# The experts' output matmuls as three F32R products of split operands

## What is computed

```python
def _L0_ffn_ref(x, A, B, Wr, br):
    router_logits = jnp.einsum('bsd,hd->bsh', x, Wr) + br
    scores = H * jax.nn.softmax(router_logits, axis=-1)
    low = jnp.einsum('bsd,hrd->bshr', x, A)
    out = jnp.einsum('bshr,hor,bsh->bso', low, B, scores)
    return SCALING * out
...
x = x + _L0_ffn_ref(_layernorm(x, axis=-1), L0_ffn_A, L0_ffn_B, L0_ffn_Wr, L0_ffn_br)
```

## Time and profile before

| | |
|---|---|
| time, median of 3 runs | 1634.19 us (1629.28 to 1638.53) |
| the profiled execution | its span 1627.3 us, 25328 instructions |
| TensorE busy | 1531.8 us (94%) |
| VectorE busy | 1129.6 us (69%) |
| ScalarE busy | 921.9 us (57%) |
| GpSimd busy | 364.1 us (22%) |
| DMA | 360.94 MB, mean 222 GB/s |

### The profile page before, as it was taken

The page is one execution under the profiler, slowest core; times in us unless marked ns, Lnnn a source line. Parts: engine busy times, 40 slices in busy tenths (PEclk is TensorE's granted clock), DMA queues, the critical chain, the costliest instruction groups (busy, mean ns, idle before and its releaser), DMA issues.

```text
span 1627.3 us, 25328 instructions
## 1 busy us (share of the span) xinstructions
PE 1531.8 (94%) x9574; PEld 1169.6 (72%) x9574; DVE 1129.6 (69%) x1782; ACT 921.9 (57%) x1702; POOL 364.1 (22%) x346
## 2 busy tenths in 40 slices
PE   7999999999999988899999999899999999999986
PEld 6567666666666656778798778798877898875554
DVE  7777745888888878644463785974776955636777
ACT  5444345888888776455543656643657644552443
POOL 1645555555433420110002000012000011001000
PEclk8999999999999999899999999999999999999998
DMA  9667677999987945356577766667766667756542
GB/s 371 204 254 243 223 181 229 276 293 284 273 233 197 253 138 189 130 185 223 202 218 233 258 226 221 214 218 232 265 233 221 223 197 237 218 180 213 203 178 104
DMA packets 127609, 360.94 MB, mean 222 GB/s; under 512 B 15744, under 2 KB 45056, under 8 KB 111872
## 3 DMA queue, kind: packets, MB, share of 16 engines
q1 hardware_dynamic: 127200, 359.19, 68.7%
q10 hardware_dynamic: 288, 0.13, 0.0%
HBM read 273.15 MB, written 86.11 MB: 221 GB/s over the span
## 4 chain that ended last, share of the span: by engine, by line
PE 74%; DVE 12%; ACT 6%; DMA 3%; issue 3%; POOL 1%; SPq 0%; DVEq 0%; ACTq 0%; POOLq 0%
PE ps L1921 21%; PE ps L1933 9%; PE ps L693 5%; PE ps L1249 5%; PE ps L1236 4%; PE ps L1272 4%; PE ps L1946 4%; PE ps L1879 3%; PE ps L1864 3%; PE ps L1809 3%; ACT a_p L1378 3%; PE ps L1824 3%; PE ps L1891 3%; DMA p_x<-in_x 2%; PE ps L652 2%
## 5 line engine op out<-in xcount | busy, mean ns | idle before, releaser
L1921 PE MATMUL ps<-m_y_split,m_win 128*128 128x512 f32 x1536 | 372.7, 396 | 2.7 <-issue 2.7
L1921 PEld LDWEIGHTS ps<-m_y_split,m_win 128*128 128x128 f32 x1536 | 284.2, 189 | 63.9 <-issue 7.1
L1308 DVE TENSOR_REDUCE a_negmax<-ps 128x1 f32<-128x640 f32 (+7 forms) x176 | 180.7, 1027 | 61.1 <-PE ps L1239 60.3
L1378 ACT ACTIVATE a_p<-ps,a_negmax 128x128 f32<-128x128 f32 (+7 forms) x256 | 188.5, 750 | 36.0 <-DVE a_negmax L1308 33.8
L1933 PE MATMUL ps<-m_wods,m_y_split 128*128 128x316 f32 x768 | 178.7, 322 | 3.8 <-DVE m_hT L2145 3.4
L2183 ACT ACTIVATE m_turned<-ps 128x512 f32<-128x512 f32 x128 | 75.0, 596 | 160.3 <-PE ps L1809 129.1
L1249 PE MATMUL ps<-ident,a_p 128*128 128x128 f32 x1152 | 157.8, 275 | 2.9 <-DVE a_pT L1321 2.0
L1236 PE MATMUL ps<-a_k,a_q 128*128 128x512 f32 (+3 forms) x384 | 124.4, 403 | 16.7 <-ACT a_p L1378 15.0
L1933 PEld LDWEIGHTS ps<-m_wods,m_y_split 128*128 128x128 f32 x768 | 128.5, 192 | 8.0 <-DVE m_hT L2145 3.7
L1249 PEld LDWEIGHTS ps<-ident,a_p 128*128 128x128 f32 x1152 | 123.5, 141 | 5.4 <-DVE a_pT L1321 3.5
L2341 POOL TENSOR_TENSOR m_scale<-m_scale,mhalf 128x2 f32<-128x2 f32 x16 | 13.0, 813 | 493.5 <-DVE m_scale L2081 493.5
(11 more groups left out here) (250 smaller groups left out, 3095.3 us busy)
## 6 DMA issues: line engine op xcount, KB each, us to landing
m_win<-mlp_in_split SPq DMA_DIRECT2D x128, 512.0 KB, 4.4
m_wods<-mlp_out_split SPq DMA_DIRECT2D x96, 316.0 KB, 3.3
p_xT<-in_xT SPq DMA_DIRECT2D x16, 1024.0 KB, 9.9
p_x<-in_x SPq DMA_DIRECT2D x16, 1024.0 KB, 10.6
a_q<-qk_split SPq DMA_DIRECT2D x64, 256.0 KB, 7.0
a_k<-qk_split SPq DMA_DIRECT2D x128, 128.0 KB, 7.2
mlp_in_split<-a_w_two SPq DMA_DIRECT2D x32, 512.0 KB, 5.5
m_hs<-in_x SPq DMA_DIRECT2D x15, 1024.0 KB, 5.6
```

The source lines that it names most:

```text
L1308: V.tensor_reduce(negmax[:, n % 4, 0:len(units[n][3])], by_head(n, score_banks(n)), AX_X, ALU.max, negate=True).then_inc(max_ready, 1)
L1378: m = S.activation(dst[:, j, :], src[:, j, :], ACT.Exp, bias=negmax[:, n % 4, j:j + 1], accum_out=rsum[:, si % 2, q * 4 + hh:q * 4 + hh + 1])
L1921: m = nc.tensor.matmul(bank_of("m", blk, step), win[s][:, wl, ic, :], y[k], start=(ic == 0 and p3 == 0), stop=(ic == HCH - 1 and p3 == 2))
```

## The change

The output matmul becomes three F32R matmuls into the same bank: copy times copy, copy times rest, rest times copy. `wB` is loaded to `wB_raw` and split once by VectorE, after its part of the last turn of block 0, into `wB_hi` and `wB_lo` (which takes the place of `wB_raw`). Per tile the turned low-rank values are split into `lT` and `lT_lo` by two VectorE instructions, which read PSUM; ScalarE's copy is gone. The places in `order` stay as they are. TensorE waits for the split weights instead of for the load. The program is made with a DMA descriptor scratch of 1024 bytes.

```diff
+        wB_hi = sb("e_B_hi", [P, D], F32R)
+        lT_lo = [sb(f"e_lowT_lo{k}", [P, P], F32R) for k in range(2)]
...
-        wB = sb("e_B", [P, D])
+        start = place[0]
+        wB_raw = sb("e_B", [P, D])
+        place[0] = start
+        wB_lo = sb("e_B_lo", [P, D], F32R)
...
-        lT = [sb(f"e_lowT{k}", [P, P]) for k in range(2)]
+        lT = [sb(f"e_lowT{k}", [P, P], F32R) for k in range(2)]
...
-                pe.wait_ge(eB_loaded, 32)
+                pe.wait_ge(tables_ready, EXPERTS)
                 wait_for_emptied(pe, "e", i, "lowT")
                 wait_for_bank(pe, "e", i, "out", q)
-                nc.tensor.matmul(bank_of("e", i, "out", q), lT[i % 2][:, :], wB[:, 512 * q:512 * q + 512],
-                                 start=True, stop=True).then_inc(eout_mm, 1)
+                for p3, (l, w) in enumerate(((lT, wB_hi), (lT, wB_lo), (lT_lo, wB_hi))):
+                    m = nc.tensor.matmul(bank_of("e", i, "out", q), l[i % 2][:, :], w[:, 512 * q:512 * q + 512],
+                                         start=(p3 == 0), stop=(p3 == 2))
+                m.then_inc(eout_mm, 1)
...
+            if part == "lowT":
+                dve.wait_ge(elwT_mm, i + 1)
+                dve.wait_ge(eout_mm, 4 * (i - 1))
+                c = dve_own.then_inc(V.tensor_copy(lT[i % 2][:, :], bank_of("e", i, "lowT")[:, 0:P]))
+                dve.wait_ge(dve_own.sem, c)
+                V.tensor_tensor(lT_lo[i % 2][:, :], bank_of("e", i, "lowT")[:, 0:P], lT[i % 2][:, :].bitcast(F32),
+                                ALU.subtract).then_inc(one.sem(("e", i, "lowT")), 1)
...
+        def split_experts():
+            dve.wait_ge(eB_loaded, 32)
+            V.tensor_copy(wB_hi[:, :], wB_raw[:, :]).then_inc(tables_ready, 1)
+            dve.wait_ge(tables_ready, EXPERTS - 1)
+            V.tensor_tensor(wB_lo[:, :], wB_raw[:, :], wB_hi[:, :].bitcast(F32), ALU.subtract).then_inc(tables_ready, 1)
...
                     turn_dve(i, q)
+                    if (i, q) == (0, 7):
+                        split_experts()
...
-            if part == "lowT":
-                act.wait_ge(elwT_mm, i + 1)
-                act.wait_ge(eout_mm, 4 * (i - 1))
-                S.activation(lT[i % 2][:, :], bank_of("e", i, "lowT")[:, 0:P], ACT.Copy).then_inc(
-                    one.sem(("e", i, "lowT")), 1)
...
-    nc = bacc.Bacc("TRN2", target_bir_lowering=False, num_devices=1)
+    nc = bacc.Bacc("TRN2", target_bir_lowering=False, num_devices=1, dynamic_dma_scratch_size=1024)
```

More of the change, by code:

```diff
@@ L532, in program @@
         MHALF, ONES1, ZEROS = 1, 2, 2
-        READ1, WSUM, WQ, MASKS, READ2, ASUM = 3, 4, 5, 7, 8, 9
+        READ1, WSUM, WQ, MASKS, READ2, EXPERTS = 3, 4, 5, 7, 8, 10
         sums_mm = sem("sums_mm")
@@ L2441, in mix_sp @@
                 elif what == "t" and (i, q) == (0, 0):
-                    move(wB[:, :], expB).then_inc(eB_loaded, 16)
+                    move(wB_raw[:, :], expB).then_inc(eB_loaded, 16)
                     move(brb[:, :], br.unsqueeze(0).broadcast_to([P, NE])).then_inc(eB_loaded, 16)
```

## The result

The changed kernel took **1643.79 us** (median of 5 runs, 1640.88 to 1646.23) and the kernel before 1634.19 (1629.28 to 1638.54 in 5 runs beside them): the ratio is 1.0064, with a 95% interval of 1.0042 to 1.0086. That is slower by 9.6 us in medians. The forecast was 1639.2 us, with most of its chance on "no difference" (slower by over 0.5% had 0.28); the result lies inside the whole range of 1627 to 1648 us, on its upper side, and 0.6 us above the forecast's own +0 to +9 us.

What follows compares the result with a forecast made beforehand. TensorE bounds 835 to 1570 us, VectorE to 1607; -7.1 + 3.5 + 1.0 + 0.6 + 0.5 + 6.2 + 0.3 = +5.0 us on the 1627.3 us span, plus 6.9 to the median: 1639.2 us, range 1627 to 1648.

Steps and rivals of the forecast that it cites:

- products, tiles 0 to 11: Output matmuls on TensorE: 41 of 48 outputs stand where TensorE is last and save 0.173 us each, -7.1 us.
- tile 2, stop and clock: TensorE waits near 1080 us for VectorE's late copy, +3.5 us; half of a 2.1 us half-speed loss behind it, +1.0.
- tile 1, tiles 5 and 6: Copies on VectorE ahead of existing TensorE waits: +0.6 us for tile 1, +0.5 us for tiles 5 and 6 together.
- tail: Last tiles: copies lengthen VectorE's work, tile 13's late copy stops TensorE and its clock falls; +6.2 us, bounds 1.2 to 8.
- split of the weights: VectorE's one-time split near 699 us fits its idle time beside GpSimd's subtractions: +0.3 us, between 0 and 2.
- layout, scratch: Smaller descriptor scratch and shifted SBUF addresses cost nothing.
- sum: All terms together: +5.0 us on the profiled span, giving 1639.2 us, +0.3%.
- rival 2: Late VectorE copies: both stops cost their clock in full, tiles 5 and 12 stop too; +10 us, 1644 us, chance 0.20.
- the prediction's own signs: In the changed profile: TensorE stops near 1080 and 1600 us, none above 0.5 behind 699, 1 to 2 ahead at 1570.
- rival 4: At the MLP's start the split and GpSimd's subtractions hold each other up; TensorE stands 2 us, 1641 us, chance 0.10.

Runs made afterwards that it cites:

- e3: The changed kernel with its F32 output matmul back and the weights unsplit, VectorE still making copy and rest: 1647.62 us beside 1635.31, ratio 1.0066.
- e5: The changed kernel with the weights' split cut into four pieces behind MLP steps of block 0: 1643.03 us beside 1634.20, ratio 1.0050.
- e1: The kernel before with the 1024-byte descriptor scratch and the new tiles laid out but unused: 1634.64 us beside 1635.31, ratio 0.9995.
- e4: The changed kernel with the two VectorE copy instructions of tiles 2, 13 and 15 earlier in VectorE's order: 1635.66 us beside 1635.31, ratio 0.9997.
- e8: The changed kernel with 12 unused matmuls ahead of tiles 2 and 13's first output, into the output's own bank: 1647.17 us beside 1634.20, ratio 1.0072.
- e9: The changed kernel with 12 unused matmuls ahead of tiles 2 and 13's first output, into the free down-product bank: 1639.88 us beside 1634.86, ratio 1.0035.
- e2: The kernel before with split weights and three products, ScalarE's copy kept and reused in the third (output wrong): 1632.24 us beside 1635.31, ratio 0.9973.

## Why the prediction came out as it did

By its own steps, predicted against the ledger:

| step | predicted | measured |
|---|---|---|
| products, tiles 0 to 11 | -7.1 | -4.4 (after against e3) |
| tile 2, stop and clock | +3.5 and +1.0 | +5.2 (e3; after +5.0: 3.4 and 1.6) |
| tile 1, tiles 5 and 6 | +0.6 and +0.5 | -0.1 and +0.7 (e3) |
| tail | +6.2 | +8.0 (after), +6.5 (e5), +7.5 (e3) |
| split of the weights | +0.3 | +1.7 |
| layout, scratch | 0 | 0 (e1) |
| 710 to 970 us, with the clock near 900 us | none | +0.7 |
| sum | +5.0 | +11.9 in the ledger; +9.6 in medians |

**The mechanism was right.** Both stops are where the prediction put them, for the reason it gave: 3.34 us at tile 2 (said 3.5) and 6.08 at tile 13 (said 5 to 6), both ended by the rest on VectorE, which stands in a stretch without a gap. e4 takes away the place alone and with it 8 to 11 us. Tiles 5 and 12, which rival 2 had stop as well, don't: only three waits at L1897 are for it, the third is tile 15's, 1.39 us. Of the prediction's own signs two failed: the wait behind the split was 1.40 us, where none above 0.5 was expected, and at 1570 us TensorE was not 1 to 2 us ahead of before but 3.9 behind (6.19 less the 2.3 of the start).

**The products were over-counted, not over-priced.** The term was 41 outputs by 0.173. One output saves 0.16 (1.29 - 1.14 gives 0.15, the matched instructions 0.15 to 0.18). 41 x 0.16 would be 6.6; 4.4 arrived. Matching against e3 says where it went, for the 47 outputs between 970 and 1569 us:

- Around tile 1's four (1000 to 1053 us) the changed kernel gains nothing and loses 0.5 us to e3. Its half-speed stretch comes behind the wait at 1043 us (clock 0.63 over 1044 to 1048 us), while e3 has 1.00 there.
- The four of tile 10 (1522 to 1535 us) gave 0.07 us together: the two waits behind them, 0.37 and 0.66 us before, are 0.67 and 0.84.
- Eight more gave nothing: one each near 1086, 1232, 1274 and 1315 us, and both near 1286 and 1480. The waits at 1285 and 1287 us grew from 0.78 and 1.24 us to 0.96 and 1.40, the one at 1318 from 0.43 to 0.74, and behind 1274 one of 0.30 us is new; near 1086, 1232 and 1480 no such wait is to be seen, and why nothing was gained there stays open.
- The other 31 at 0.16 are 5.0 us, less the 0.5 of tile 1.

The prediction knew the long VectorE stretches (7 outputs lost) and missed the short ones. Nor did the prediction see that at tile 1 the turn L1814 needs the bank of the low-rank values, and so waits 1.54 us for L2130; the later wait for L2060 gives most of that back (2.66 us, before 3.80).

**Clock.** At tile 2 I took half of 2.1; 1.6 came in the changed kernel and 2.7 in e5. In every profiled execution with a bare stop of 3.3 us there (after, e3, e5, e8) the clock was at half speed behind it. The full price is the likelier of the two for this stop, and rival 2's half of the argument was the better one. It is no law for every stop: near 900 us all eleven profiled executions have a stop of 2.73 us, and the clock fell behind it in four (after, e4, e8, e9) and in none of the other seven. Those four are among the five that run the whole split at 702 us beside GpSimd (e2 is the fifth). Whether the split has to do with it, 200 us later, no run settles, so this +1.6 us may belong to the changed kernel and not to one execution.

**Tail.** The router of tile 14 (L2102, before L2095) started at 1619.99, 12.5 us later than before; less the 6.19 that TensorE was behind at 1569, that is 6.3, against 3.9 + 2.1 said. What was mis-sized is what follows: nothing was to be lost there, and 1.7 us were. Behind tile 15's wait of 1.39 us the clock fell in this execution:

```profile
1631.00:1635.00 4.00, 3.25 (x8) 2.57 (x9) 1.93 (x5) 0.00 (x0) 0.00 (x0) 0.64 0.64 264
```

In e5, with the same order at that place, the same stretch has 1.00, and its whole tail costs 6.5 us. e8 and e9 have the same wait of 1.39 us and 1.00 over that stretch as well. So this part comes in some executions (one of these four) and not in others.

**The split.** This step failed, and rival 4 was right. The prediction had argued that TensorE needs only the last subtraction near 703 us and that no row before 835 us shows the engines held up. The second was a misreading: the trace of before has such rows, this one with GpSimd's instruction at 2.13 us, where the median of its 16 is 0.70:

```profile
651.64 1.75 DVE L2021 TENSOR_TENSOR m_hs<-m_hs,m_first_A 128x1536 f32<-128x1536 f32 x1
651.82 2.13 POOL L2341 TENSOR_TENSOR m_scale<-m_scale,mhalf 128x2 f32<-128x2 f32 x1 [7.96 <-DVE m_scale L2081]
```

In the changed kernel it costs time: GpSimd 5.53 us instead of 2.54, VectorE 3.27 instead of 2.29, TensorE +1.70. By the Trainium skill, "SBUF — State Buffer", section "Who interferes with whom", a VectorE instruction with two SBUF inputs and a GpSimd instruction that reads SBUF exclude each other for a whole instruction; the trace agrees (the second GpSimd subtraction takes 3.32 us instead of 1.3 beside VectorE's), and e5 agrees as well, with 2.55 us and no wait once the VectorE subtraction stands elsewhere. The price by that rule, 2 us, was within 0.3 of the measured one; the +0.3 from the idle time alone was not.

**The sum.** The distance of 6.9 us between +5.0 and +11.9 is 2.7 (products) + 1.4 (split) + 1.8 (tail) + 0.7 (tile 2) - 0.5 (tiles 1, 5 and 6) + 0.7 (710 to 970 us), within 0.1. Without the last and without the 1.5 us of clock in the tail the ledger is at +9.7, and the medians say +9.6. That nearness proves little: the clock in the tail comes in one execution of four, but the one near 900 us may be the changed kernel's own, and the execution of before lies below its median by more than its 2.3 us at the start. In the terms of the rivals the result is rival 2's total by another sum: the late copies nearly as forecast, the lock of rival 4 on top, and a smaller gain.

## What to carry to other kernels

When an edit moves a small step to another in-order engine, the price is not its 0.6 us but its place: look at what stands ahead of it there, at whoever waits, and at the clock behind the stop. Moving three such steps by a few lines was worth 8 to 11 us, where the 7.7 us that 48 outputs save by count gave 4.4. Count a saving on the busiest engine only up to its next wait for a stretch that doesn't move, short waits included. If an edit adds a long VectorE instruction on SBUF operands where GpSimd is at work, look for another time for it, or cut it into pieces and put those where GpSimd is idle.

## What the runs showed of the hardware

- Three F32R products of 128x512 start 0.23 to 0.24 us apart and replace one F32 matmul at a gain of 0.14 to 0.18 us. Each of the 192 has its own weight load in the trace, and e2, where the weights stay the same, gains no more (0.16) than the changed kernel, where they change once. The first stands 0.14 us behind the F32R matmul of 316 columns ahead of it.
- A VectorE copy and a two-input subtraction of 128x2048 in SBUF beside two GpSimd subtractions of 128x512: the GpSimd pair takes 5.53 us instead of 2.54, one 2.26 beside the copy and one 3.32 beside the subtraction, and VectorE's subtraction 3.27, against 2.29 for an addition of that shape.
- Unused matmuls in a stop kept TensorE at 2.4 GHz behind it in e9 and more than paid: with 24 of them the kernel was 4 to 5 us faster than the changed one, 3.9 of them at the two stops. Written to a bank that is not yet read out they wait for the same thing as the work behind them, and cost 2.7 us more at tile 2.
- Profiled executions differ by several us before the work in question begins: at 697 us, ahead of every edited instruction, ten of them (one of each kernel) are 0.9 to 6.6 us behind that of before. So spans of single profiles can't be compared to better than that, while matched instructions of two traces could be to 0.02 us.
